# Interaction network layer 1 in fp16 passes, with product sums partly added by DMA

## The reference

```
out[n, o, e] = relu( sum_ij  xi[n, i, e] * x0[n, j, e] * W[i*48 + j, o] + b[o] )
```

## Time and profile before

| | us |
|---|---|
| median of 3 runs | 2483.61 |
| lowest, highest | 2477.33, 2484.41 |
| profiled execution | 2483.18 |
| its span | 2481.3 |
| busy in it: TensorE | 2371.5 |
| VectorE | 2253.5 |
| ScalarE | 2003.9 |
| GpSimd | 2005.8 |

### The profile page before, as it was taken

The page is one execution under the profiler, slowest core; times in us unless marked ns, Lnnn a source line. Parts: engine busy times, 40 slices in busy tenths (PEclk is TensorE's granted clock), DMA queues, the critical chain, the costliest instruction groups (busy, mean ns, idle before and its releaser), DMA issues.

```text
span 2481.3 us, 67324 instructions
## 1 busy us (share of the span) xinstructions
PE 2371.5 (96%) x13024; PEld 1300.3 (52%) x13024; DVE 2253.5 (91%) x9408; ACT 2003.9 (81%) x7526; POOL 2005.8 (81%) x2006
## 2 busy tenths in 40 slices
PE   1399999999999999999999999999999999999998
PEld 0255555555555555555555555555555555555553
DVE  3589999999999999999999999999999999999995
ACT  1578888888888888888888888888888888888884
POOL 7178888888788888888878888888877777777773
PEclk7699999999999999999999999999999999999999
DMA  5000000000000000000000000000000000000000
GB/s 168 5 11 11 11 11 11 11 11 9 10 10 11 11 10 12 11 11 11 9 9 11 12 11 11 11 11 12 9 9 9 9 10 9 10 9 8 9 10 3
DMA packets 113451, 34.36 MB, mean 14 GB/s; under 512 B 107860, under 2 KB 111575, under 8 KB 113400
## 3 DMA queue, kind: packets, MB, share of 16 engines
q1 hardware_dynamic: 107256, 30.73, 5.6%
q0 software_dynamic: 6144, 3.16, 0.9%
HBM read 12.82 MB, written 0.00 MB: 5 GB/s over the span
## 4 chain that ended last, share of the span: by engine, by line
PE 93%; DVE 1%; issue 0%; DMA 0%; SPq 0%; ACT 0%; DVEq 0%
PE y L430 79%; PE m L420 11%; PE m L409 3%; DVE acc L746 1%; PE m L485 0%; PE y L485 0%; PE y L492 0%; DMA xT<-lo 0%; DVE ends L746 0%; PE y L498 0%; DVE msum L755 0%; DVE ends L760 0%; DVE pooled L799 0%; SPq L263 0%; DVE mp L779 0%
## 5 line engine op out<-in xcount | busy, mean ns | idle before, releaser
L430 PE MATMUL y<-whi,xT 128*128 128x512 f16 x6144 | 1990.3, 379 | 11.2 <-DMA xT<-lo 8.1
L528 ACT ACTIVATE work<-y,xc 128x128 f32<-128x128 f32 x5632 | 1597.3, 378 | 368.1 <-PE y L430 332.4
L746 DVE SCALAR_TENSOR_TENSOR acc<-y,xc,acc 128x128 f32<-128x128 f32 x5632 | 1680.5, 342 | 67.7 <-PE y L430 50.0
L324 POOL TENSOR_TENSOR part<-part,work 128x512 f32<-128x512 f32 x896 | 1138.1, 1270 | 204.7 <-ACT work L528 122.2
L430 PE MATMUL y<-wlo,xT 128*128 128x512 f16 x3072 | 1164.6, 379 | 0.0
L430 PEld LDWEIGHTS y<-whi,xT 128*128 128x128 f16 x6144 | 600.5, 98 | 633.6 <-issue 25.4
L430 PEld LDWEIGHTS y<-wlo,xT 128*128 128x128 f16 x3072 | 300.8, 98 | 241.0 <-issue 0.6
L420 PEld LDWEIGHTS m<-wsq,work 128*128 128x128 f32 x2304 | 355.1, 193 | 103.8 <-issue 20.0
L320 POOL TENSOR_TENSOR part<-work 128x512 f32<-128x512 f32 x256 | 326.6, 1276 | 61.8 <-ACT work L528 58.8
L420 PE MATMUL m<-wsq,work 128*128 128x128 f32 x2304 | 366.2, 278 | 2.5 <-DVE zst L725 2.5
L286 POOL DMA_INDIRECT emb<-tbl,ids_sb x192 | 185.4, 966 | 43.6 <-issue 27.2
(11 more groups left out here) (102 smaller groups left out, 1131.2 us busy)
## 6 DMA issues: line engine op xcount, KB each, us to landing
xT<-hi SPq DMA_TRANSPOSE x256, 2.2
xT<-lo SPq DMA_TRANSPOSE x256, 2.3
xx<-w SPq DMA_DIRECT2D x4, 768.0 KB, 5.4
emb<-tbl,ids_sb POOLq DMA_INDIRECT x192, 2.4
work<-w SPq DMA_DIRECT2D x4, 768.0 KB
x0T<-x0hl SPq DMA_TRANSPOSE x128
wt_sb<-W_top SPq DMA_DIRECT2D x1, 768.0 KB
w1s<-w_pair SPq DMA_DIRECT2D x1, 640.0 KB
```

The lines of the kernel that those rows point to most:

```text
L324: pool.tensor_tensor(a[:], a[:], p[:, m, :], ALU.add).then_inc(s, 1)
L430: ins = nc.tensor.matmul(dst[:], xT[layer][:, parity, a, :], w[layer][:, cols], start=i == 0, stop=i == 2)
L528: nc.scalar.activation(prods[layer][:, a, k * P:(k + 1) * P], bank[:, k * P:(k + 1) * P], ACT.Copy, scale=xc[layer][:, parity, j:j + 1]).t ...
L746: ins = nc.vector.scalar_tensor_tensor(dst, y, col, mine, ALU.mult, ALU.add)
```

## The change

Layer 1: `zT` is kept and a second square `zh` in fp16 is written of the same pair sums; `squares_lo` on GpSimd writes `zl` = `zT` - `zh` in fp16 (128 x 1152). The weights are split into `w1h`, `w1l` in the setup. `layer1` runs nine passes zh x w1h, nine zh x w1l, the stacked product, and nine zl x w1h: 28 fp16 passes, 5 or 6 a piece, with a wait for `zl` before pass 20.

Sums: of the first four product banks, a DMA issued by GpSimd adds banks 2 and 3 onto banks 0 and 1 (two banks at once, 512 KB, fp32, SBUF to SBUF). `sum_rest` adds banks 4 and 5 of layer 2; `sum_all` waits for the DMA and adds the rest and the two DMA-made banks, then folds. The DMA of one layer is issued before the sums of the other. ScalarE may write a tile's products only once all sums of the tile before are done.

Order: `relu(1)`, `scale(1)`, `hi_part(1)`, `columns(1)`, `lo_part(1)`, `over_e(1)` and both merges move to later banks, the transposes of layer 3's input to the next step and to the front of SP's step. GpSimd's loops are written out. In the setup the layer-1 arrays are loaded first, their work stands around the maxima of W2 and W3, and both scales are made by one chain.

```diff
-SUMS = [n + 1 for n in NA]
+SUMS = [n - 1 for n in NA]
+ADDED = 2
...
-W1_SETUP = 7
+W1_SETUP = 8
+KF = KT - 1
+L1_PASSES = 3 * KF + 1
...
-        wst, zst = sb("wst", [P, P], f16), sb("zst", [P, P], f16)
+        w1h, w1l = sb("w1h", [P, KT, P], f16), sb("w1l", [P, KF, P], f16)
+        zh, zl = sb("zh", [P, KF, P], f16), sb("zl", [P, KF, P], f16)
+        wst, zst = w1h[:, KF, :], sb("zst", [P, P], f16)
...
             sp.dma_start(ids_sb[:], ...)
+            sp.dma_start(w1s[:], w_pair).then_inc(s_in, 16)
...
             for l, w in enumerate((w2, w3)):
...
-            sp.dma_start(w1s[:], w_pair).then_inc(s_in, 16)
...
+            sp.dma_start(sel[:], select).then_inc(s_sel, 16)
...
-                t0, t1, t2 = v + 3, v + 2, v + 1
+                t0, t1, t3 = v + 3, v + 2, v
+                if active(t3):
+                    transpose_x(1, t3, parity)
                 if active(t0):
                     transpose_x0(t0, 1 - parity)
                 if active(t1):
                     transpose_x(0, t1, parity)
-                if active(t2):
-                    transpose_x(1, t2, 1 - parity)
...
-            def sums(layer, tile):
-                s, done = s_sum[layer], tile * SUMS[layer]
+            def written(layer, tile, m):
+                wait(pool, s_prod[layer], tile * PRODS[layer] + (m + 1) * Q)
+            def add_by_dma(layer, tile):
+                p = prods[layer]
+                written(layer, tile, 2 * ADDED - 1)
+                pool.dma_start(p[:, 0:ADDED, :], p[:, ADDED:2 * ADDED, :], accum_op=ALU.add).then_inc(s_dma[layer], 16)
+            def sum_rest(layer, tile):
+                wait(pool, s_sum[layer], tile * SUMS[layer])
+                for m in range(2 * ADDED + 1, NA[layer]):
+                    written(layer, tile, m)
+                    pool.tensor_tensor(part[layer][:], prods[layer][:, m - 1, :], prods[layer][:, m, :],
+                                       ALU.add).then_inc(s_sum[layer], 1)
+            def sum_all(layer, tile):
+                s, n = s_sum[layer], tile * SUMS[layer] + NA[layer] - 2 * ADDED - 1
                 p, a = prods[layer], part[layer]
-                def written(m):
-                    wait(pool, s_prod[layer], tile * PRODS[layer] + (m + 1) * Q)
-                wait(pool, s, done)
-                written(1)
-                pool.tensor_tensor(a[:], p[:, 0, :], p[:, 1, :], ALU.add).then_inc(s, 1)
-                for m in range(2, NA[layer]):
-                    written(m)
-                    wait(pool, s, done + m - 1)
-                    pool.tensor_tensor(a[:], a[:], p[:, m, :], ALU.add).then_inc(s, 1)
-                n = NA[layer] - 1
-                wait(pool, s, done + n)
+                wait(pool, s_dma[layer], (tile + 1) * 16)
+                if NA[layer] == 2 * ADDED + 1:
+                    written(layer, tile, 2 * ADDED)
+                wait(pool, s, n)
+                for m in range(ADDED):
+                    rest = p[:, 2 * ADDED, :] if m == 0 and NA[layer] == 2 * ADDED + 1 else a[:]
+                    pool.tensor_tensor(a[:], rest, p[:, m, :], ALU.add).then_inc(s, 1)
+                    n += 1
+                    wait(pool, s, n)
                 pool.tensor_tensor(a[:, 0:2 * P], a[:, 0:2 * P], a[:, 2 * P:4 * P], ALU.add).then_inc(s, 1)
-                wait(pool, s, done + n + 1)
+                wait(pool, s, n + 1)
                 wait(pool, s_m[layer], tile)
                 pool.tensor_tensor(psum[layer][:], a[:, 0:P], a[:, P:2 * P], ALU.add).then_inc(s, 1)
+            def squares_lo(t):
+                wait(pool, s_zts, t * 3 + 3)
+                pool.tensor_tensor(zl[:], zT[:, 0:KF, :], zh[:], ALU.subtract).then_inc(s_zl, 1)
...
+                t0, t2, t3 = v + 3, v + 1, v
+                if active(t3 - 1):
+                    sum_all(1, t3 - 1)
+                if active(t2):
+                    add_by_dma(0, t2)
                 if parity == 0 and active(v + 4):
                     x0_scaled(v + 4)
-                gather(b, fields[0:1])
-                if active(v + 1):
-                    sums(0, v + 1)
+                gather(b, fields)
                 if parity == 0 and active(v + 4):
                     x0_lo(v + 4)
-                gather(b, fields[1:2])
+                if active(t2):
+                    sum_rest(0, t2)
+                    sum_all(0, t2)
+                if active(t3):
+                    add_by_dma(1, t3)
+                if active(t0):
+                    squares_lo(t0)
                 if columns:
                     spread(b, *columns)
-                if active(v):
-                    sums(1, v)
+                if active(t3):
+                    sum_rest(1, t3)
             for v in range(-4, 1):
                 step(v, v % 2)
...
                     for e in range(0, E, SPREAD):
                         step(v, v % 2, b + 1, columns=(e, SPREAD))
                         v += 1
-                    end = (b + 1) * E
-                else:
-                    end = TILES - 6
-                with pool.Fori(0, (end + 1 - v) // 2) as pair:
-                    step(pair * 2 + v, 1)
-                    step(pair * 2 + v + 1, 0)
-            for v in range(TILES - 5, TILES):
-                step(v, v % 2)
+                while v < min((b + 1) * E + 1, TILES):
+                    step(v, v % 2)
+                    v += 1
+            sum_all(1, TILES - 1)
...
+            l1_passes = [(zh, w1h, k) for k in range(KF)] + [(zh, w1l, k) for k in range(KF)] + \
+                [(zst, wst, None)] + [(zl, w1h, k) for k in range(KF)]
             def layer1(t, c):
                 if c == 0:
                     wait(pe, s_zts, t * 3 + 3)
                     wait(pe, s_zst, t + 1)
-                for k in (2 * c, 2 * c + 1):
-                    z, w = (zT[:, k, :], wsq[:, k, :]) if k < KT - 1 else (zst[0:STACK, :], wst[0:STACK, :])
-                    ins = nc.tensor.matmul(misc[0][:, 0:P], z, w, start=k == 0, stop=k == KT - 1)
-                if 2 * c + 2 == KT:
+                for i in range(L1_PASSES * c // 5, L1_PASSES * (c + 1) // 5):
+                    if i == 2 * KF + 1:
+                        wait(pe, s_zl, t + 1)
+                    z, w, k = l1_passes[i]
+                    z, w = (z[0:STACK, :], w[0:STACK, :]) if k is None else (z[:, k, :], w[:, k, :])
+                    ins = nc.tensor.matmul(misc[0][:, 0:P], z, w, start=i == 0, stop=i == L1_PASSES - 1)
+                if c == 4:
...
-                wait(act, s_sum[layer], (t - 1) * SUMS[layer] + max(a, 1))
+                wait(act, s_sum[layer], t * SUMS[layer])
...
+                    wait(act, s_zl, t)
+                n = min(4, KF - 4 * g)
...
+                nc.scalar.activation(zh[:, 4 * g:4 * g + n, :].rearrange("p t c -> p (t c)"),
+                                     misc[PAIR_BANK[g]][:, 0:n * P], ACT.Square, scale=SQUARE)
...
-                    if n == 17 and active(t2):
+                    if n == 22 and active(t2):
                         relu(1, t2)
-                    if n == 21 and active(t2):
-                        hi_part(1, t2)
-                        columns(1, t2, other)
+                    if n == 1 and active(t3):
+                        hi_part(1, t3)
+                        columns(1, t3, parity)
...
-            dve.wait_ge(s_in, 7 * 16)
+            dve.wait_ge(s_in, 6 * 16)
...
+            raw_max(0)
+            dve.wait_ge(s_wpe, 2)
             dve.wait_ge(s_setup, 2)
             nc.vector.scalar_tensor_tensor(wsq[0:F, 0, :], misc[0][0:F, 0:P], ...)
...
+            raw_max(1)
...
+            nc.vector.tensor_copy(w1h[:], wsq[:]).then_inc(s_setup, 1)
...
+            nc.vector.tensor_tensor(w1l[:], wsq[:, 0:KF, :], w1h[:, 0:KF, :], ALU.subtract).then_inc(s_setup, 1)
...
-                        if n == 5 and active(t3 - 1):
+                        if n == 3 and active(t3):
                             if k == 0:
-                                merge(1, t3 - 1, 0)
-                            if k == 2:
-                                merge(1, t3 - 1, 1)
+                                lo_part(1, t3)
+                            if k == 1:
+                                over_e(1, t3)
                         if n == 3 and k == 3 and active(t1):
                             pre1(t1, parity)
                         if n == 7 and active(t1):
                             scale(0, t1, k)
+                        if n == 9 and k % 2 == 0 and active(t3 - 1):
+                            merge(1, t3 - 1, k // 2)
                         if n == 9 and active(t1):
                             if k == 1:
                                 lo_part(0, t1)
...
                                 over_e(0, t1)
                         if n == 11 and k == 0 and active(t3 - 1):
                             over_e(2, t3 - 1)
-                        if n == 16 and active(t2):
-                            if k == 1:
```

(17 more changed lines are left out.)

77 lines of the change are left out of this document (31 added, 46 removed).

## The result

The changed kernel takes 2490.78 us (2490.13 to 2491.79, 7 runs) against 2483.02 us (2477.33 to 2484.41, 7 runs) beside it: ratio 1.0034 [1.0023, 1.0046]. It is slower by a little, where 2434 was forecast. And this ratio flatters it. On four other chips the kernel before took 2460 us; the profile taken on one of them shows that a long wait of its setup is missing there. The changed kernel took 2490.93 us on that chip too, ratio 1.0127 [1.011, 1.0144]. So two things have to be explained: a setup that gained 23 us only where the kernel before has that wait, and a loop that lost 25 us instead of gaining 54 (forecast 61, less 7).

The account below looks back on a forecast made before the run. TensorE, busy throughout the loop, was taken as the bound. From 2483.2 us: layer 1 -61, gathers +7, tail +5, fill +4, setup -4 gave 2434 us, range 2400 to 2520.

Parts of the forecast that it names:

- Layer 1, -61: TensorE's layer-1 pieces: 28 fp16 passes cost 1.61 us a tile instead of 2.09, saving 61 us over 128 tiles.
- Its waits for TensorE cover that.: ScalarE: three more squares a tile, 1.5 us, fit into its 2.6 us a tile of waiting for TensorE.
- nothing charged: SP: layer 3's transposes go first; those of x0 and layer 2 come behind, needed a half step later: no cost.
- GpSimd, +7: GpSimd's tiles with gathers: late sum_all delays merge and squares_lo, charged 0.2 us on 36 even tiles.
- L: Accumulating DMA, issue to landing: 4.4 us, midway between 3.8 (bytes counted once) and 5.1 (twice); GpSimd's round breaks even at 4.85.
- a wait of part for the DMA: GpSimd's sums: a wait of this sort in the profile would show the forecast wrong; no size given.
- Ends: Program's ends: layer 3's last sum +4 and layer 2's chain +1 at the tail; pipeline fill +4 us.
- Setup, -4: Before the loop: the 34 us hold keeps its length but starts earlier; first x0 scale at 87 instead of 91 us.
- the first rival: Setup hold gone, first x0 scale at 68 us: 23 us off instead of 4, 2415 us; chance 0.12.
- The gain stays in the consumers: Loop: VectorE or GpSimd's round replaces TensorE as bound, returning 0.2 to 0.5 us a tile: about 2470 us; chance 0.17.
- Slower by the accumulating DMA: sum_all's wait: DMA landing after 5.6 us makes GpSimd's round 19.2 us a tile: 2618 us; chance 0.18.
- the weight-load rival: Layer 1 on TensorE: weight loads pace the new passes at 0.086 us each, 2.4 us a tile: 2535 us; chance 0.03.

Follow-up runs that it names:

- pair of mended kernels: mended, and the same kernel with layer 1 as before (fp32 halves, one set of squares, no squares_lo): 2408.54 and 2460.52 us.
- g2_bank: Changed kernel with the third group of pair sums put into the other bank, misc[1]: 2476.05 us, ratio 1.0065 to the kernel before.
- no_zh: Changed kernel with the fp16 copy of the squares not written in the loop, a constant in its place: 2463.28 us, ratio 1.0012.
- mended: Changed kernel with third group in misc[1], x0's transpose first, layer 2's merge at bank 22 behind the stacked low part, one gather per flight: 2408.54 us, ratio 0.9797.
- merge22: g2_x0t with both halves of layer 2's merge at bank 22, behind the stacked low part: 2418.53 us.
- merge22_split: merge22 with one gather in each of GpSimd's two flights instead of two in the first; same kernel as mended: 2407.98 us.
- merge_late: g2_x0t with the merge's first half behind bank 20's last fma and its second in bank 22: 2436.84 us, ratio 0.991.
- g2_x0t: Changed kernel with the third group of pair sums in misc[1] and x0's transpose sent ahead of layer 3's: 2475.12 us, ratio 1.0064.
- before_again: The kernel before, unchanged, profiled again on a further chip: 2460.5 us.
- tiny_dma: Changed kernel with the accumulating DMA adding 32 columns (16 KB) instead of 1024 (512 KB), products not summed fully: 2564.48 us, ratio 1.0422.

## Why the prediction was wrong

Against the kernel before of the same chip the spans differ by 7.2 us: the first bank ends 22.9 us earlier, the loop takes 127 x 0.201 = 25.5 us more, and the tail 4.6 us more. The forecast failed in the loop, in two steps that it had charged at nothing or next to nothing: ScalarE's second squares, and what a late psum holds.

**Layer 1, -61.** The mechanism was right, the size a little high. The pair of mended kernels measures 52 us. The pieces fell from 2.04 to 1.63 us a tile (5.29 and 4.88 less five banks of 0.65); the forecast had 2.09 to 1.61. A pass takes 0.056 us in groups of five and six, as the pair sums had shown (0.0575). By the rule of the Trainium skill (TensorE: Matmul & The Clock Gate, Back-to-back issue gap) of 81 ns it would have been 0.7 us a tile more, an estimate that no trace here bears out.

**ScalarE: the first step that failed.** "Its waits for TensorE cover that." They did in sum: ScalarE is busy 1793 of 2000 us. But TensorE waits for a particular square. The second square of a group stands directly ahead of a bank's release, and the third group of pair sums, next in TensorE's fixed order, wants that bank: 0.39 us a tile at bank 17 against 0.48 saved. A sum of idle time is no cover for an instruction with a date. g2_bank and no_zh both close this wait.

**SP: "nothing charged" for x0's transpose.** Wrong by 0.19 us a tile at bank 12. The step was moved behind two issues of 1.1 and 1.2 us and behind their wait for the low part of layer 3's input. Undone alone it brings 2 us, since bank 17 takes its place.

**GpSimd, +7: the second step that failed, and the larger.** L was forecast as 4.4 us and is 4.7; the round fits 17.74 us, as mended shows, so L lay on the right side of the break-even of 4.85. From 16 KB to 512 KB landing grows by 4.7 - 2.2 = 2.5 us, against the forecast's 1.36 for loading such bytes: near the end of "bytes twice", an estimate, since no run has a plain copy of the same shape. It agrees with the Trainium skill's rule on a DMA's add (Collectives: The Full Stack, The bandwidth ceiling). The +7 for the gathers was near what moving one of them gave back, 10 us from merge22 to merge22_split. What was missed is what a late psum holds. "Behind the late sum_all stand merge on VectorE and squares_lo", the text says, and charges 0.2 us on 36 tiles. merge stood in the middle of bank 20, so psum held a PSUM bank and with it TensorE: merge_late against g2_x0t, 38 us. no_zh shows that with ScalarE's step out of the way the rest still ate the whole gain: 2463.3 us against 2460.0 of the kernel before beside it. The forecast's sign, "a wait of part for the DMA", was no sign: mended has the same wait. squares_lo took 2.72 us (2.65 forecast), and TensorE waited for zl once in the stretch 300 to 2300 us, 0.2 us.

**Ends.** Tail +5: from the last tile's first bank to the end 62.4 us against 57.8 in the kernel before and 58.6 in before_again, +4.6 and +3.8. Fill +4: from the first x0 scale to the first y 18.2 against 17.8 and 18.1 us, next to nothing. But the first two full steps after it take 28.4 and 19.6 us where the kernel before has 25.3 and 18.2 (mended 24.6 and 17.7); these 4.5 us are part of the loop's 25.5. Since mended has none of them, they go with the waits above rather than with "more squares and zl in the open"; that they come near the forecast's 4 is luck.

**Setup, -4.** The first x0 scale came 23 us earlier on the chip with the hold, at 67.75 us where the first rival had 68, and no earlier on the others. The forecast took one unexplained wait of one profile for a property of the kernel.

**The rivals.** "The gain stays in the consumers" (0.17) was the nearest in place, with 128 x 0.2 to 0.5 us returned; what came back was 0.69 (0.49 saved in the pieces, 0.20 lost in all). Each wait hides behind the next: mended singly, transpose, merge and third group give 2, 16 and 15 us; in sequence, third group 15, transpose 1, merge 38, stacked low part 18, gathers 10. "Slower by the accumulating DMA" had the sign, but not the cause: it needed an L of 5.1 us or more. The sum of the weight-load rival comes to 2534, not 2535.

## What to carry to other kernels

Before counting idle time as cover, list for every instruction added ahead of a semaphore who waits for that semaphore next in a fixed order; here 0.5 us added before a release took 0.39 us a tile of the 0.48 saved elsewhere. Do not let an instruction that still has to wait for another engine stand between the parts of work that frees a shared buffer: that cost 0.3 us a tile here. Moved behind the bank it held the next thing that someone needed, the stacked low part. In mended it stands inside a bank again, two banks later, and costs almost nothing, since psum is there by then (0.7 us of waits in 2000). A long wait that nobody else waits behind, as GpSimd's for its transfers, can stay. And when several such waits are suspected, mend them together before judging any one, for alone they show a fraction of their worth.

## What the hardware showed that was not expected

- VectorE's two tensor_scalar steps between two-column SBUF tiles take 0.17 and 0.21 us in the changed kernel, and up to the rest of GpSimd's running add of 1.3 to 1.6 us beside it (means of 0.86 and 1.16 us in tiny_dma); moved by four banks they are at 0.31 and 0.18. The Trainium skill (SBUF — State Buffer, Who interferes with whom) has this as an exclusive lock on a shared port; the trace agrees, and adds that two columns are enough to lose most of an add's time.
- The same 20 fp32 matmuls release VectorE after 3.3 us on one chip and after 33.2 us on another, behind the same setup; 23 us of the whole program hang on it. Why is not known.
- A gather lands after 2.4 us in the kernel before. Issued 1 to 2 us after a 512 KB transfer in mended it lands after 3.9 us, and 3 to 4 us after one, in 2.5 us. Behind a 16 KB transfer it takes 2.5 us wherever it stands (medians, loop alone).
